# Tile-wise normalisations with BN statistics, and a subtraction moved from GpSimd to VectorE

## What is computed

```python
# twice: the end of an attention layer (d = 128, eight heads of 16)
agg = jax.ops.segment_sum((att[..., None] * v).reshape(-1, d), rows, num_segments=n)
out = agg + embeds
mu = jnp.mean(out, axis=-1, keepdims=True)
var = jnp.mean((out - mu) ** 2, axis=-1, keepdims=True)
return (out - mu) / jnp.sqrt(var + 1e-06) * ln_s + ln_b

# once: the router (four heads, four experts)
e = leaky_relu(a_src[src] + a_dst[dst], negative_slope=0.2)
ee = jnp.exp(e - e_max[dst])
denom = segment_sum(ee, dst)
agg = segment_sum(h[src] * (ee / denom[dst])[:, :, None], dst)
```

## Time and profile before

| | us |
|---|---|
| median of three runs (7080.81 to 7087.0) | 7081.17 |
| the profiled execution | 7074.46 |
| its span | 7072.6 |
| first VectorE operation of `between` to its last kv store's issue | 2780.9 to 2872.7 |
| first VectorE operation of `leave` to the issue of its row store | 4939.0 to 5104.2 |
| `neighbour_sum`, its clearing to its last addition | 6582.0 to 6928.1 |

### The profile page before, as it was taken

The page is one execution under the profiler, slowest core; times in us unless marked ns, Lnnn a source line. Parts: engine busy times, 40 slices in busy tenths (PEclk is TensorE's granted clock), DMA queues, the critical chain, the costliest instruction groups (busy, mean ns, idle before and its releaser), DMA issues. The chain is left out here.

```text
span 7072.6 us, 118162 instructions
## 1 busy us (share of the span) xinstructions
PE 5305.6 (75%) x28073; PEld 4149.9 (59%) x28073; DVE 5250.9 (74%) x15782; ACT 3459.6 (49%) x9814; POOL 4748.6 (67%) x5326
## 2 busy tenths in 40 slices
PE   5995677777777776667666676666679999999781
PEld 2664555566666665456665665665456666666671
DVE  7994677688888888577777777777667777777776
ACT  0002667666666665566666666665322222222561
POOL 1441777777777775677777777776377777777781
PEclk7557899877777777887777878777578888888555
DMA  1005444444444443454545445444423222322437
GB/s 29 4 4 137 139 140 140 139 130 129 131 129 130 130 131 108 127 138 132 138 131 137 132 132 138 132 132 118 103 49 65 59 59 60 60 63 58 127 120 193
DMA packets 502729, 769.54 MB, mean 109 GB/s; under 512 B 119802, under 2 KB 365657, under 8 KB 502061
## 3 DMA queue, kind: packets, MB, share of 16 engines
q0 software_dynamic: 198048, 441.63, 23.9%
q1 hardware_dynamic: 292961, 308.36, 16.0%
q10 hardware_dynamic: 11052, 12.00, 0.7%
HBM read 689.74 MB, written 71.83 MB: 108 GB/s over the span
## 5 line engine op out<-in xcount | busy, mean ns | idle before, releaser
L706 POOL DMA_INDIRECT att_kv_e<-kv,gnn_idx x3240 | 3108.9, 960 | 1131.9 <-issue 929.7
L791 PE MATMUL att_ps_sum<-att_vals,att_hot 128*125 128x136 f32 x6480 | 1237.0, 347 | 902.9 <-DVE att_vals L849 900.5
L791 PEld LDWEIGHTS att_ps_sum<-att_vals,att_hot 128*125 128x125 f32 x6480 | 1062.4, 238 | 1104.0 <-DVE att_vals L849 1080.5
L777 PE MATMUL att_ps_q<-qs,att_hot_t 125*128 x6480 | 1178.3, 340 | 265.6 <-ACT att_hot_t L823 260.2
L706 POOL DMA_INDIRECT max_rows<-rows,gat_idx x1128 | 1066.0, 945 | 421.1 <-issue 339.4
L777 PEld LDWEIGHTS att_ps_q<-qs,att_hot_t 125*128 125x128 f32 x6480 | 1064.9, 248 | 356.9 <-issue 355.3
L870 DVE TENSOR_TENSOR acc<-acc,att_ps_sum 125x136 f32 x3240 | 938.3, 290 | 265.8 <-DVE acc L870 174.3
L836 DVE TENSOR_TENSOR att_prod<-att_ps_q,att_kv_e 128x512 f32<-128x512 f32 x810 | 556.6, 687 | 764.1 <-issue 432.5
L808 ACT ACTIVATE att_hot<-node_no,gnn_loc 128x125 f32<-128x125 f32 x3240 | 1014.4, 384 | 0.0
L2437 DVE CUSTOM_DVE_ANT_0 max_junk<-max_far,max_ps_b 125x256 bf16<-125x256 bf16 x2256 | 792.4, 416 | 260.8 <-PE max_ps_b L2401 260.8
L801 ACT ACTIVATE att_ps_dve<-att_clipped 128x32 f32<-128x32 f32 x810 | 161.4, 199 | 1396.8 <-DVE att_clipped L857 1395.6
(11 more groups left out here) (454 smaller groups left out, 7971.0 us busy)
## 6 DMA issues: line engine op xcount, KB each, us to landing
att_local<-gnn_loc_rows SPq DMA_DIRECT2D x810, 128.0 KB
att_kv_e<-kv,gnn_idx POOLq DMA_INDIRECT x3240
max_local<-gat_loc_rows SPq DMA_DIRECT2D x282, 128.0 KB
gs_local<-gat_loc_rows SPq DMA_DIRECT2D x141, 256.0 KB, 3.3
outs<-ex_y SPq DMA_DIRECT2D x25, 896.0 KB
max_rows<-rows,gat_idx POOLq DMA_INDIRECT x1128, 2.4
X<-in_x SPq DMA_DIRECT2D x10, 1120.0 KB
ans_late<-outs SPq DMA_DIRECT2D x11, 896.0 KB
```

What stands on the lines that cost most here:

```text
L706: pool.indirect_dma_start(rows(j, e), None, source, bass.IndirectOffsetOnAxis(ap=g.idx[:, t:t + 1], axis=0))\
L777: ins = pe.matmul(ps_q[j % 2][:, e * D:(e + 1) * D], hot_t[:, j % 2, e * LANES:(e + 1) * LANES], at(qs, numbers.of(k * GROUP + e)), start= ...
L791: ins = pe.matmul(sum_of(u, i), hot[:, g_of % SLOTS, e, :], vals[:, g_of % VALS, e, :], start=True, stop=True)
```

## The change

Three edits. In `Norm.vector` the six passes over a chunk become, for each of its tiles, one BN statistics operation, one fused subtraction of the mean and multiplication by the scale, and one fused multiplication by the reciprocal root and addition of the shift. The mean and the sum of squares come from the two halves that the statistics give, by seven operations on 125 x 10 elements. Each tile gives a signal of its own when it is done; TensorE waits for its tile, GpSimd for the tenth of the chunk. In `neighbour_sum` the piece `less` moves from GpSimd's list to VectorE's, between the second addition and `near_hot`.

```diff
-        chain(dve.tensor_reduce(mean, E, AX, ALU.add))
-        chain(dve.tensor_scalar(mean, mean, 1.0 / D, None, ALU.mult))
-        chain(dve.tensor_tensor(E, E, each(mean, D), ALU.subtract))
-        chain(dve.tensor_tensor(self.tmp[:], E, E, ALU.mult))
-        dve.tensor_reduce(var, self.tmp[:], AX, ALU.add).then_inc(m["var_ready"], 1)
+        for t in tiles:
+            last = dve.bn_stats(self.stats[:, t], self.E[:, t])
+        chain(last)
+        dve.tensor_tensor(mean, stats[:, :, 1], stats[:, :, 4], ALU.add)
+        chain(dve.tensor_tensor(gap, stats[:, :, 1], stats[:, :, 4], ALU.subtract))
+        dve.tensor_tensor(var, stats[:, :, 2], stats[:, :, 5], ALU.add)
+        chain(dve.tensor_tensor(gap, gap, gap, ALU.mult))
+        dve.tensor_scalar(mean, mean, 0.5, None, ALU.mult)
+        chain(dve.tensor_scalar(gap, gap, D / 4.0, None, ALU.mult))
+        dve.tensor_tensor(var, var, gap, ALU.add).then_inc(m["var_ready"], 1)
         if i == 0:
             dve.wait_ge(m["w_in"], 32)
-        chain(dve.tensor_tensor(E, E, over(self.s[:], CHUNK), ALU.mult))
+        for t in tiles:
+            last = dve.scalar_tensor_tensor(out=self.E[:, t], in0=self.E[:, t], scalar=at2(self.mean, t), in1=self.s[:],
+                                            op0=ALU.subtract, op1=ALU.mult)
+        chain(last)
         dve.wait_ge(m["root_ready"], i + 1)
         chain(dve.reciprocal(var, var))
-        chain(dve.tensor_tensor(E, E, each(var, D), ALU.mult))
-        dve.tensor_tensor(E, E, over(self.b[:], CHUNK), ALU.add).then_inc(m["normed"], 1)
+        for t in tiles:
+            dve.scalar_tensor_tensor(out=self.E[:, t], in0=self.E[:, t], scalar=at2(self.var, t), in1=self.b[:],
+                                     op0=ALU.mult, op1=ALU.add).then_inc(m["normed"], 1)
...
-                pool.wait_ge(normal.m["normed"], i + 1)
+                pool.wait_ge(normal.m["normed"], (i + 1) * CHUNK)
...
-                pe.wait_ge(normal.m["normed"], t // CHUNK + 1)
+                pe.wait_ge(normal.m["normed"], t + 1)
...
-            def less(k, r, j):
-                pool.wait_ge(m["leaky"], k + 1)
-                pool.tensor_tensor(e_sb[:, k % 4], e_sb[:, k % 4], info[:, k % 4, :, FH:2 * FH], ALU.subtract)\
-                    .then_inc(m["less"], 1)
-            steps(pool, [(0, sums), (-1, less), (-2, weigh), (-3, rest_of), (-4, low)])
+            steps(pool, [(0, sums), (-2, weigh), (-3, rest_of), (-4, low)])
...
+            def less(k, r, j):
+                dve.wait_ge(m["leaky"], k + 1)
+                dve.tensor_tensor(e_sb[:, k % 4], e_sb[:, k % 4], info[:, k % 4, :, FH:2 * FH], ALU.subtract)\
+                    .then_inc(m["less"], 1)
...
-            steps(dve, [(0, gather_info), (-6, add_sum(0)), (-1, leaky), (-6, add_sum(1)), (2, near_hot), (-6, add_sum(2)),
+            steps(dve, [(0, gather_info), (-6, add_sum(0)), (-1, leaky), (-6, add_sum(1)), (-1, less), (2, near_hot), (-6, add_sum(2)),
                         (-6, add_sum(3)), (-6, load_tiles)])
```

More of the change, by code:

```diff
@@ L2025, in __init__ @@
         self.s, self.b = sb("s", [NODE_TILE, D]), sb("b", [NODE_TILE, D])
-        self.mean, self.var = sb("mean", [NODE_TILE, E.shape[1]]), sb("var", [NODE_TILE, E.shape[1]])
-        self.tmp = sb("tmp", [NODE_TILE, CHUNK, D])
+        self.mean, self.gap, self.var = (sb(n, [NODE_TILE, E.shape[1]]) for n in ("mean", "gap", "var"))
+        self.stats = sb("stats", [NODE_TILE, E.shape[1], 6])
         self.m = sem_set(nc, st, name, ["w_in", "var_ready", "root_ready", "normed"])
@@ L2035, in vector @@
         m, a = self.m, slice(i * CHUNK, (i + 1) * CHUNK)
-        E, mean, var = self.E[:, a], self.mean[:, a], self.var[:, a]
+        E, mean, gap, var, stats = self.E[:, a], self.mean[:, a], self.gap[:, a], self.var[:, a], self.stats[:, a]
+        tiles = range(i * CHUNK, (i + 1) * CHUNK)
         sums, weights = self.acc[:, a, 0:D], self.acc[:, a, D:SUMS]
```

## The result

| | before | after |
|---|---|---|
| median us (runs side by side, 8 each) | 7081.87 (7068.5 to 7087.0) | 7103.47 (7095.8 to 7113.1) |
| profiled execution, its span | 7074.46, 7072.6 | 7113.05, 7111.3 |
| first to last opening reduction of the neighbour sum | 324.9 | 360.9 |
| chunk of ten tiles in `between` | 14.86 | 12.62 |
| first transpose behind the stage's first VectorE operation, `between` and `leave` | 15.09, 15.09 | 10.49, 10.60 |

The ratio is 1.0033 (95% interval 1.0023 to 1.0042): slower by 21.6 us, 0.3%, more than the 0.2% that a measurement of this kernel can tell. The prediction said 7100.

The account below looks back on a forecast made before the run. VectorE was taken to set the neighbour sum's pace. 7074.5 - 9 - 6.6 + 34.4 = 7093.3 us; the median stands 6.7 above the profiled run, so 7100 us. Range 7057 to 7108, the forecast's own 7090 to 7108.

Parts of the forecast that it names:

- the long step: Neighbour sum: every second step takes 2.67 us instead of 2.04, because VectorE loads eight tile numbers into registers.
- Less is held by weigh: Neighbour sum: VectorE's moved subtraction starts at 0.83 us, waits for GpSimd's product and ends at 1.12.
- Rest goes first, hot falls behind it: Neighbour sum: GpSimd's operation after its product is served before VectorE's one-hot comparison, which ends at 1.80 us, today 1.57.
- no steps split: Rival, neighbour sum: steps divide between both serving orders, about +0.09 us a step, 7083 us; chance 0.18.
- The border that the prediction names: Neighbour sum: the lead that decides which of VectorE and GpSimd is served first, put between 0.05 and 0.07 us.
- hot overtakes rest: Rival, neighbour sum: VectorE's one-hot comparison is served before GpSimd's next operation, steps 1.99 or 2.62 us, 7062 us; chance 0.17.
- less isn't held: Rival, neighbour sum: the moved subtraction costs 0.10 us without waiting, steps 1.88 and 2.51, some -18 us, 7047 us; chance 0.15.
- The size of the loss: Neighbour sum: 0.23 us per step over 141 steps, with corrections +34 us, bounds 29 and 38.
- A chunk of 12.75 us, the first tile after 10.4: Both normalising stages: ten tiles take 12.75 us instead of 14.86, the first ready after 10.4 instead of 14.9.
- What the stages gain: Normalising stages: 9 us between the attentions, bounds 5 and 12; 6.6 us behind the second, bounds 4 and 7.5.
- the 2.2 us at the roots: Stage behind the second attention: 2.2 of 2.5 us of later waits at ScalarE's roots would be gained.

Follow-up runs that it names:

- e5: Kernel before with only the normalisations changed and four tile numbers loaded each step, ahead of the fourth addition, instead of eight every second step: 7034.40 us, ratio 0.9940.
- e4: The changed kernel with the moved subtraction taking zeros from PSUM instead of the maximum from SBUF: 7056.31 us, 0.9970 of the kernel before.
- e8: The changed kernel with one unused 128x32 addition per step on GpSimd where its subtraction stood: 7072.29 us, 0.9993 of the kernel before.

## Why the prediction was right, step by step

*What bounds the sum.* Right: VectorE's list sets the pace, and the long step is the load of tile numbers. e5 shows it by taking the load out of the way.

*Less is held by weigh.* Right: 0.292 us median against an expected 0.29, starting at 0.83. e4 and e8 show that it is the meeting of the two engines, not the instruction. The rule of the Trainium skill (SBUF — State Buffer, SBUF: two separate sides), an exclusive lock taken by a VectorE operation with two SBUF inputs, agrees with e4: 0.29 us with two SBUF inputs and 0.18 with one, in the same place.

*Rest goes first, hot falls behind it.* Right: 766 ns median against an expected 0.76, steps of 2.28 and 2.91 against 2.27 and 2.90. The rest at 0.49 and low at 0.68 also came as said, and no steps split. The border that the prediction names for the kernel before, 0.05 to 0.07 us, is not what its trace shows: of 116 weighs whose record starts 0.042 to 0.049 us behind hot's, 107 were served first and 9, at 0.045 to 0.049, were not (hot 0.48, weigh 0.70). To be served first, hot had to start at least 0.045 us ahead there. Here rest starts 0.006 to 0.017 us ahead of hot, in all but one of the 123 steps in which the two meet, so by this border the order was not close. What no row had told is whether VectorE keeps its turn when less is released, the point on which the rival "hot overtakes rest" hung. The prediction gave it 0.17 against 0.50; the runs settle it, and that this came out as forecast is in part luck. The rival "less isn't held" gave 1.88 and 2.51 us for a case that this kernel is not; e4 made it one, and has 1.88 and 2.51 (6706.94, 6709.45, 6711.33), with 14 us less in the sum where the rival said 18.

*The size of the loss.* +36.0 us in the trace against +34.4, inside 29 to 38. (The terms as written, 32.4 + 4.6 - 3, make 34.0; no row gives the 0.4 more.) The moved operation takes 0.18 us on VectorE where nothing holds it and took 0.25 on GpSimd. The Trainium skill (GPSIMD Engine Reference, Key points) has VectorE about twice as fast at elementwise work; the rows have 1.4 times, and the move still cost 36 us.

*A chunk of 12.75 us, the first tile after 10.4.* Right: 12.62 and 10.49. The terms, start to start, were 3.97 us for the first four operations (expected 3.98), 2.07 for the statistics (2.13), 0.96 for the small operations (0.89), 2.74 and 2.63 for the fused ones (2.8 and 2.7), 0.25 for the reciprocal. By the setup of some 150 cycles in the Trainium skill (VectorE: DVE Perf Modes, Side-by-side) the estimate was 0.30 us for each tile operation and a chunk of 14.1; the rows have 0.20 and 0.27 (ten in 2.03 and in 2.70) and 12.62, so that setup does not stand in full between two operations of a kind here.

*What the stages gain.* The term that was too large. From the stage's first VectorE operation to the first gather of the second attention, `between` takes 95.5 us in three profiles of the old normalisation (95.3 to 95.8) and 88.5 in nine of the new one with tile-wise signals (86.6 to 90.1): 7.0 us, not 9. The first tile carries 4.6 of it; from the first transpose to the last it takes 69.3 us instead of 71.9, so behind the first tile the stage gains 2.6 us where 4.5 had been taken (49 tiles at 1.41 us each, the slow end of the 1.34 to 1.41). In `leave` the first tile comes 4.5 us sooner, but from the first transpose to the last it takes 119.3 us in three old profiles (118.1 to 120.9) and 119.2 in nine new ones (117.7 to 121.3). To the store of the rows the stage takes 156.1 us instead of 160.6: 4.5 us less, not 6.6. The step that failed here is the 2.2 us at the roots: those waits did go (ScalarE waits for VectorE's variance once, 14.4 us, where it did five times, 20.0), and the stage didn't get shorter by them. They were not on its path. In `between` the store of keys and values takes back what the transposes gain, as said (29.1 us of waiting instead of 21.7), and some more than said; the new wait of VectorE for the root, 3.5 us, belongs there, and lies late, in the fourth chunk (15.08 us instead of 12.62). How much of the missing 2 us is the root's and how much the store's was not tried.

*The sum of it.* 7.0 and 4.5 us less, 36.0 more: +24.5 by the traces, +21.6 and +23.3 by the two comparisons, +18.8 predicted. Of the 5.7 us between the first and the last, 4.1 are the stages' gain and 1.6 the loss. The medians of before were 7074 to 7082 in the four comparisons, so the absolute 7103.5 carries a few us of that as well.

## What to carry to other kernels

Ask of an operation moved to VectorE not what it costs there, but what GpSimd is doing at that moment and what comes next in VectorE's list: a held operation of 0.18 us pushed one of 0.48 behind another of GpSimd's and cost 0.24 us a step, and the same operation two places further down its list cost nothing, so that what GpSimd was relieved of could come out as a gain. Place small work where the engine waits for its own result anyway; in this loop that gap of 0.21 us took in four register loads that had cost 0.3 us elsewhere. Of a stage's gain from a faster engine the first tile was the part that came as reckoned (4.5 us in both stages); of the later waits, reckoned at 4.5 and 2.2 us, 2.6 and nothing came. That a wait disappears doesn't show that it lay on the path.

## What the runs showed of the hardware

- Adding an operation to GpSimd made the loop faster: weigh at 0.86 instead of 0.66 of the step, and with it less at 0.19 instead of 0.29 us and hot at 0.65 instead of 0.77.
- Four loads of tile numbers in a wait of 0.21 us added nothing (the additions 0.42 us apart with them, 0.41 without), where eight made a step 0.63 us longer. That was expected only in part.
- Who comes first at the meeting of the two engines was stable over the stage with less ahead of hot: 141 hots at 766 ns median and 769 at most, with rest's record starting 0.006 to 0.017 us ahead of hot's. It was not in the kernel before: with weigh's record 0.045 to 0.049 us behind hot's, some steps served the one first and some the other.
- Ten statistics of 125x128 take 2.03 us and ten fused operations of that size 2.70, start to start 0.19 and 0.26 us, where the record of each single one is 0.28 and 0.35.
